# Attention stage, one step of ScalarE: the two exponentials of a step now stand ahead of the copy of the high parts

## The reference

```
Q = (q @ Wq.T + bq) ; K = (k @ Wk.T + bk) ; V = (v @ Wv.T + bv)     # 4 batches, 16 heads of 16
scores = einsum('bhqd,bhkd->bhqk', Q, K) / sqrt(16)
scores = where(mask == 1, -1e9, scores)
attn   = softmax(scores, axis=-1)
out    = einsum('bhqk,bhkd->bhqd', attn, V) ; return out @ Wo.T + bo
```

## Time and profile before

| | before |
|---|---|
| median of three executions | 1335.86 us |
| the profiled execution, its own time | 1331.35 us |
| its span in the profile | 1329.6 us |
| granted TensorE clock over the span | 0.953 |
| busy: TensorE | 1168.6 us |
| busy: VectorE | 883.1 us |
| busy: ScalarE | 693.5 us |
| busy: GpSimd | 383.7 us |

### The profile page before, as it was taken

One profiled execution on the slowest core, in us unless ns is written; L12 is line 12 of the kernel. 1 busy time (PEld: TensorE's weight loads), 2 busy tenths in 40 slices (PEclk: granted clock), 3 DMA queues, 4 the chain that ended last, 5 costly groups with the idle time before them and its releaser, 6 DMA issues. The chain is left out here.

```text
span 1329.6 us, 20495 instructions
## 1 busy us (share of the span) xinstructions
PE 1168.6 (88%) x6928; PEld 1015.2 (76%) x6928; DVE 883.1 (66%) x1667; ACT 693.5 (52%) x1045; POOL 383.7 (29%) x373
## 2 busy tenths in 40 slices
PE   3878759988879979969999989999999999688987
PEld 2666648777768869969999978778788788577876
DVE  6778664656545545635655453999989998675675
ACT  2122214555533334434444233887988988665755
POOL 2400027112141600600500044512522621992130
PEclk9988779998889989989999999999999999898999
DMA  8100001002336243252321023321422323210001
GB/s 291 64 0 0 0 8 64 0 5 68 68 60 150 83 132 95 60 155 95 92 94 68 1 71 96 103 69 47 127 71 64 113 83 99 74 33 5 13 26 43
DMA packets 66853, 92.84 MB, mean 70 GB/s; under 512 B 15440, under 2 KB 32592, under 8 KB 66640
## 3 DMA queue, kind: packets, MB, share of 16 engines
q1 hardware_dynamic: 65152, 89.67, 22.9%
q10 hardware_dynamic: 1616, 2.10, 0.5%
HBM read 80.45 MB, written 11.14 MB: 69 GB/s over the span
## 5 line engine op out<-in xcount | busy, mean ns | idle before, releaser
L1824 DVE CUSTOM_DVE_ANT_0 at_pr<-at_sc,at_mk 128x512 f32<-128x512 f32 x256 | 165.5, 684 | 32.3 <-PE at_sc L2046 31.6
L1730 ACT ACTIVATE at_pr<-at_pr,at_nmx 128x512 f32<-128x512 f32 x256 | 170.3, 716 | 19.2 <-DVE at_nmx L1824 18.6
L1961 DVE TENSOR_TENSOR W_1l<-at_pt,W_1h 128x1024 fp32r<-128x1024 f32 x128 | 155.8, 1217 | 12.3 <-ACT W_1h L1725 12.0
L2061 PE MATMUL at_pt<-ident,at_pr 128*128 128x128 f32 x1024 | 137.1, 278 | 21.7 <-DVE W_1l L1961 21.0
L1725 ACT ACTIVATE W_1h<-at_pt 128x1024 fp32r<-128x1024 f32 x128 | 130.7, 1021 | 41.8 <-PE at_o L2080 39.9
L2061 PEld LDWEIGHTS at_pt<-ident,at_pr 128*128 128x128 f32 x1024 | 116.9, 143 | 45.2 <-issue 20.1
L315 DVE TENSOR_TENSOR moe_ms<-moe_hs,moe_gate 128x512 f32<-128x512 f32 x112 | 86.3, 771 | 90.7 <-ACT moe_hs L282 56.5
L282 ACT ACTIVATE moe_hs<-moe_hid,cols 128x512 f32<-128x512 f32 x128 | 88.0, 688 | 103.8 <-PE moe_hid L167 102.9
L274 ACT ACTIVATE moe_hh<-moe_ms 128x512 fp32r<-128x512 f32 x112 | 70.8, 632 | 133.7 <-DVE moe_ms L315 133.7
L301 DVE TENSOR_TENSOR moe_hl<-moe_ms,moe_hh 128x512 fp32r<-128x512 f32 x112 | 87.2, 779 | 69.1 <-ACT moe_hh L274 69.1
L2080 PE MATMUL at_o<-W_1h,at_vaug 128*128 128x512 f32 x256 | 113.8, 444 | 3.0 <-ACT at_hs L1644 2.2
(11 more groups left out here) (315 smaller groups left out, 3320.2 us busy)
## 6 DMA issues: line engine op xcount, KB each, us to landing
moe_gate<-expert_weights SPq DMA_DIRECT2D x224, 128.0 KB, 2.9
w_stage<-in_ew SPq DMA_DIRECT2D x8, 1024.0 KB, 6.4
at_kp<-at_heads SPq DMA_DIRECT2D x96, 64.0 KB, 2.7
at_qp<-at_heads SPq DMA_DIRECT2D x96, 64.0 KB, 2.7
w_stage<-in_w SPq DMA_DIRECT2D x4, 1024.0 KB, 9.5
f_gate<-expert_weights SPq DMA_DIRECT2D x32, 128.0 KB, 3.0
w_stage<-in_mask SPq DMA_DIRECT2D x16, 256.0 KB, 3.9
at_rb<-at_recip SPq DMA_DIRECT2D x64, 64.0 KB, 2.0
```

Of the source, the lines that this page charges most:

```text
L1730: act.activation(pr_of(t)[:, x, :], pr_of(t)[:, x, :], ACT.Exp, bias=nmx[:, t % 4, x:x + 1], scale=-1.0).then_inc(s["ex"], 1)
L1824: dve.tensor_tensor_reduce(pr_of(t)[:, x, :], SB[x][:, :], mk[u // 2 % 2][:, j, :], -float(HD) ** -0.5, 3.0e38, ALU.add, ALU.min, nmx[:, t ...
L1961: dve.tensor_tensor(PH[1][:, n % 2, :], PT[n % 2][:, :, :].rearrange("p c q -> p (c q)"), f(PH[0][:, n % 2, :]), ALU.subtract).then_inc(s[ ...
L2061: last = pe.transpose(PT[t % 2][:, c, j * P:(j + 1) * P], pr_of(t - i + j // 2)[:, j % 2, kc * P:(kc + 1) * P], g.ident[:, :])
```

## The change

In each step of ScalarE's program the block of the high part of step t-3 and the block of the two exponentials of step t change places. Nothing is added or taken out, and every wait and signal stays at its instruction. The programs of the other engines are the same row by row.

```
                     if u == 0 and st == 13:
                         act.wait_ge(s_wo, 96)
                         act.activation(WOH, wost[:, :, :], ACT.Copy).then_inc(s_woh, 1)
+                    if 0 <= u < UNITS:
+                        for x in range(2):
+                            act.wait_ge(s["tt"], 2 * t + x + 1)
+                            act.activation(pr_of(t)[:, x, :], pr_of(t)[:, x, :], ACT.Exp, bias=nmx[:, t % 4, x:x + 1],
+                                           scale=-1.0).then_inc(s["ex"], 1)
                     if 0 <= n < STEPS * UNITS:
                         act.wait_ge(s["tr"], n + 1)
                         if n >= 2:
                             act.wait_ge(s["pv"], n - 1)
                         act.activation(PH[0][:, n % 2, :], PT[n % 2][:, :, :].rearrange("p c q -> p (c q)"), ACT.Copy)\
                             .then_inc(s["ph"], 1)
-                    if 0 <= u < UNITS:
-                        for x in range(2):
-                            act.wait_ge(s["tt"], 2 * t + x + 1)
-                            act.activation(pr_of(t)[:, x, :], pr_of(t)[:, x, :], ACT.Exp, bias=nmx[:, t % 4, x:x + 1],
-                                           scale=-1.0).then_inc(s["ex"], 1)
                     if st == 0 and u >= 1:
                         high_o(3 * (u - 1))
```

More of the change, by code:

```diff
@@ L1726, in _ @@
                             .then_inc(s["ph"], 1)
[L1727 to L1731, removed]
                     if st == 0 and u >= 1:
```

## The result

The changed kernel takes **1472.83 us** (median of four runs, 1469.51 to 1476.24) against 1333.19 us for the kernel before on the same chip (four runs, 1330.07 to 1337.21): a ratio of **1.1034**, 95% interval 1.0992 to 1.1075, or 10% slower. The forecast was 1469 us.

The account below looks back on a forecast made before the run. TensorE, VectorE and ScalarE were all taken as nearly full at 3.17 us a step; the change makes a ring of 4.14 us. 120.9 + 9.6 + 2.8 = +133.3 us on 1335.86 gave 1469 us, range 1453 to 1496.

Parts of the forecast that it names:

- The ring: Attention step: maximum, exponentials, high part, low part, next maximum in one chain of waits; 4.14 us against 3.17, +120.9 us.
- VectorE's work behind the low part: Reciprocals, norm statistics and norm applications there lengthen the step by their whole length, together +9.6 us.
- the cover of 1.79 us: VectorE's wait for the high part behind the second maximum; work placed there ahead of the low part costs nothing.
- The two steps with `ffn_turn`: Unit 7, where VectorE waits for that copy ahead of the low part: 5.53 us each, +2.8 us for both.
- What the sum took as nothing, with 3 us either way: Column sums of unit 7 and both ends of the attention stretch: about nothing together, 3 us either way.
- The end: Three last attention steps, with no exponentials or projection to wait for; counted within about nothing, 3 us either way.
- Profile and median: Base of the forecast: the profiled 1331.35 us lay 4.5 us under the median, so +133.3 went onto 1335.86.
- A: Rival: distances above 4.14 us today keep their length (GpSimd in unit 6, column sums in unit 7); 1482 us, chance 0.14.
- the prediction's own sign (5 us): Wrong about the long steps if units 6 and 7 take more than 16 x 4.14 us plus 5.
- B: Rival: TensorE's clock falls in the attention, steps up to 0.46 us longer; 1497 us if half of them, chance 0.20.
- C: Rival: not slower, transposes no longer wait for exponentials and the high part is in time; 1316 us, chance 0.02.
- D: Rival: same time, the copy moves into ScalarE's idle time and TensorE bounds the step; 1336 us, chance 0.02.

## Why the prediction was right

**The ring** was right in mechanism and in size. The sum had 4.14 us for a step, measured are 4.14 and 4.15 in nearly all steps without extra work. The waits came as foretold too: 115 for the high part, 173.3 us, where about 120 and 180 to 200 us were expected, and TensorE is busy 70% of the stretch. Only the distance from low part 1 to 125 lies outside its 520 to 530 us. All four parts of the ring came out of single rows of the old trace; that worked here because the same wait was the last in step after step, with hardly any spread. The first rows of each part must be of instructions that had waited, though, or stood behind no other: the distance of two starts on a full engine says nothing on the handoff.

**VectorE's work behind the low part**, 9.6 us in the sum, measured 8.4: the reciprocals cost 0.10 each and not 0.16, some 2.1 us for all; the statistics 1.82 and the applications 1.38 with their reciprocal. When they were moved ahead of the low part, 7.1 us of this went; the statistics and an output sum together passed the cover of 1.79 us.

**The two steps with `ffn_turn`**, +2.8 us: right by mechanism (5.55 us for the first, and 5.54 and 5.53 without the disturbance), too small for the second, which took 7.11 us. TensorE ran at a low clock in that step:

```profile
1340.00:1344.00 4.00, 3.65 (x15) 3.00 (x16) 1.42 (x5) 2.24 (x3) 3.79 (x3) 0.65 0.00 0
```

The clock had been low once before, in the step behind the stretched norm application, ahead of which TensorE was idle for 3.18 us. In the two kernels where the application took 1.38 us both steps with `ffn_turn` are 5.52 to 5.55. But the kernel with the even steps changed had 7.11 us as well, with an application of 1.84 us. So the low clock as the cause of the 7.11 is read from the trace, and what brings it down in that step is not shown.

**What the sum took as nothing, with 3 us either way**, was the term that failed. The stage is 534.9 us where the sum had 525.8. The missing 9 us, by the distances above 4.14: the three subtractions of unit 0, 2.9 us; the stretched application, 1.5; the statistics of the feed-forward norm, which with an output sum beside it pass the cover, 0.7; the second `ffn_turn`, 1.6; the column sums, 0.7 and 2.5. That is 9.9 us, less the 1.2 us of reciprocals and norm work that were priced too high; the step at the low clock (0.2) and the hundredths of the bare steps (0.3) close the sum. Of the 2.9 us, 1.8 are the subtractions and 1.1 the hold-up by GpSimd. The column sums cost the same 3.2 us in the kernel in which the signs wait, so GpSimd is not their cause; TensorE works on them partly at the low clock in both. I had not looked at what stands ahead of the maxima on VectorE, though it is as much on the ring as what stands behind the low part.

**The end** gave 1.3 us back, which the sum had left in its "about nothing": the first step without exponentials is 1.74 us instead of 3.56, the next 4.34 instead of 3.84.

**Profile and median.** I had added the difference to a median of 1335.86. The new median of before is 1333.19 and the difference of medians 139.6 us, against 133.3 forecast, so the sum was 5% too small. From 1333.19 the same sum gives 1466.5, 6.3 us under the result. That 1469 stands only 3.8 us under it is luck of the base.

**The rivals.** A (long steps stay long, 1482) did not come in unit 6, whose distances are 4.14 to 4.25 us: GpSimd was indeed outlasted. Unit 7 took 76.2 us, 9.9 more than 16 x 4.14, so by the prediction's own sign (5 us) it was wrong about the long steps there. But only the column sums are long steps that stayed; the rest is `ffn_turn`, which the sum had, and statistics, a hold-up and a low clock, which it did not have. B (the clock, 1497) did not come over the steady part: 0.99, with one step of 4.36 us. It was near, though: with half of the products the clock was 0.90, with 0.52 us more of idle time 0.92. It came in two places of unit 7, at a cost of a few microseconds. The rule on short idle times that was set beside it ("TensorE: Matmul & The Clock Gate" in the Trainium skill) does not show in the steady part of the changed kernel, with 1.7 us of idle time in a bare step; the two kernels at 0.90 and 0.92 agree with it, and there it costs no time in the bare steps. C and D (1316 and 1336) would have needed slack in the ring, and there was none: 0.52 us more on it cost 62 us, half a microsecond beside it nothing.

## What to carry to other kernels

Where two engines hand work to each other, write down for each the order of its program and follow the arrows: if engine A waits for B's work of this step, and B's work of this step stands behind something that waits for A, the step is as long as the sum around the ring, however idle both are. Work of an earlier step that is ready belongs ahead of work that must wait for this step. The price of such a ring can be read off the old trace by single handoffs; then look at every instruction that stands on the ring, not only at the one that was moved.

## What the runs showed of the hardware

VectorE and GpSimd hold each other up when both work in SBUF: a subtraction of 128 x 512 took 1.77 us instead of 0.68 beside a product of GpSimd, four norm applications 3.37 instead of 1.38 beside two products, and with GpSimd held back they took 1.38 again. It works the other way round too. Behind the attention of the changed kernel GpSimd's subtraction (L1509) started at 1411.28 us, 0.07 us after two additions of VectorE with a subtraction behind them, and took 2.95 us; in the attention the same instruction takes 1.3.

The Trainium skill, "SBUF — State Buffer", section "Who interferes with whom", says that the two share a pair of ports as an exclusive lock: the one that starts first has it for its whole instruction, and the other blocks. It says so for VectorE instructions with two inputs in SBUF, against a GpSimd instruction that reads SBUF, and for those in a two-port mode. The subtraction is of the first kind, and the trace agrees: 1.22 us were left of GpSimd's product when it started, and it is 1.09 us longer. In which mode the applications ran no trace tells. Not every instruction of GpSimd blocks them in this way: beside its first sign (`TENSOR_SCALAR`, 1.93 us) the same four applications took 1.67 us in the kernel before. VectorE's statistics and its low part, which reads one of its inputs from PSUM, kept their 1.40 and 1.22 us beside GpSimd.

TensorE's granted clock was 0.99 in the steady part of the changed kernel, where it is idle for 1.7 us in each bare step, 0.92 with 0.52 us more of idle time in each step, and 0.90 with half of the products. None of this moved the distance of bare steps by more than 0.01 us, but for the one step of 4.36. A lower clock of an engine that waits is no cost until its work passes the ring.
